# Other places for the side jobs of a unit, a re-ordered prologue, and gating and shared expert moved ahead in the last stages of an attention and mixture-of-experts layer

## The chip, the core and the metric

The kernel runs as one program on one core of one Trainium2 chip. The metric is the device time of one execution in microseconds (us). The engines are named as the profile names them: PE is TensorE (matmuls; its weight loads have a row of their own, PEld), DVE is VectorE, ACT is ScalarE, POOL is GpSimd, SP is SyncE, whose queue issues nearly all DMAs.

## The reference

One layer on x of 2048 tokens by 128 channels, all float32. The modulation rows sa, ca, ga, sb, cb, gb come from silu(c) @ wmod.

```python
h = layernorm(x) * (1 + ca) + sa
x = x + ga * attention(h)       # 16 heads; head n is tokens 128n..128n+127, reshaped to 2048 rows of 64
h = layernorm(x) * (1 + cb) + sb
x = x + gb * ffn(h)

# attention of a head: xq, xk, xv = h_block @ w.T, seen as 2048 x 64 each
out = softmax(xq @ xk.T / 8) @ xv           # then projected by wo

# ffn: gate by sigmoid(h @ gate_w.T) + expert_bias, top 2 of 8 experts, each token weighted by its score
# ahead of the expert and behind it; plus one shared expert for all tokens
h_e = (silu((w * h) @ w1[e].T) * ((w * h) @ w3[e].T)) @ w2[e].T * w
shared = silu(h @ sw1.T) * (h @ sw3.T) @ sw2.T
```

## The kernel before

The program is written engine by engine, each an in-order stream, tied by semaphores. It is fully unrolled and has three stages.

**Prologue.** Weights are loaded and transposed on PE (the setup jobs, list `SETUP`, copied out of PSUM by ACT), layer norm statistics of all 16 blocks of x are made by DVE, the first head is projected, and the first 20 "pairs" are done. A pair is a matmul of queries by keys into two PSUM banks (L1060) and a maximum over it on DVE (L870). The maxima give each row's softmax shift (`peak`, transposed on PE at L1071, stored by DVE, and spread by a DMA into `shifts`).

**Units.** Each of 16 heads has two halves of 1024 queries; a half is a unit, numbered 0 to 31. A unit has 32 places, four to a step. At the first two places of a step PE makes the scores of one key tile each (six matmuls of fp32r in row tiles of 64, L1113 to L1119), at the other two it multiplies an earlier tile of exponentials by v (L1137, fp32 in column tiles). ACT makes the exponentials (L738), POOL adds them up (L789, 15 adds of 128x1024 in a unit), which is the denominator. At set places there are side jobs for the next head or unit, written in the tables `LONG_JOBS`, `LOW_PLACES` and `SCALE_PLACES`, one dictionary for the first half and one for the second: q, k, v projections of the next head, a `sum` of the denominators of the unit before, its reciprocals on DVE in four parts (`inv`, L890) and the product with them (`scale`), the output projection `out` (L1161) of the head before, and `shift`. Twelve pairs of the next unit stand at the odd places 1 to 23, four of the unit after at 25 to 31. All side jobs on PE but the pairs use one PSUM bank, so each waits for the one before to be read out (`job_free`). In `side_jobs` the long jobs are put in first and the pairs behind them:

```python
    places = [[] for _ in range(4 * PAIRS)]
    for place, (kind, i) in LONG_JOBS[half].items():
        ...
    if pairs:
        for i in range(EARLY_PAIRS, PEAK_PAIRS):
            places[2 * (i - EARLY_PAIRS) + 1].append(("pair", i))
```

All pairs of the units use the same two banks, so a pair's matmul waits until DVE has reduced the one before.

**The last head and the feed-forward stage.** The last head (units 30 and 31) has no next head to project. In unit 31 DVE does the second layer norm of the 12 blocks that are ready (statistics, L322 for the normalization), PE transposes them (`turn`), makes the gate logits, and DVE picks the experts (`gate`, L492 to L509). Then come 36 items (4 groups of 512 tokens by 8 experts and, last of its group, the shared one). For each routed item PE spreads a row of token weights over all partitions by a matmul with a selecting matrix (`spread`, L391), ACT copies it out (`keep_spread`), POOL multiplies the tokens by it (L412), PE does w1 and w3 (L442, L443), ACT silu (L474), DVE two products (L532, L534), PE w2 (L424). The last four blocks' norm, gate and weights are done between items 2 and 8.

## Time and profile before

| | us |
|---|---|
| three runs | 1463.69, 1469.81, 1469.3 |
| median of them | 1469.3 |
| the profiled execution | 1464.93 |
| its span | 1463.1 |
| PE busy in the span | 1397.1 |
| POOL busy | 1186.8 |
| DVE busy | 929.7 |
| ACT busy | 679.9 |
| mean granted TensorE clock | 0.981 of full speed |

The span is what the profiler saw from the first instruction to the last; 1.8 us of the profiled execution's time lie around it. PE's busy time is near the span, but matmuls are pipelined and their ends are modelled, so it does not say that PE has nothing to give. The gaps between weight loads (PEld) are the finer tool.

### The profile page before, as it was taken

Reading aid. Unit: us, or ns where it says so; the run is one execution under the profiler, and the core shown is the slowest. Engines: PE = TensorE matmul, PEld = TensorE weight load, DVE = VectorE, ACT = ScalarE, POOL = GpSimd, SP = SyncE. Lnnn points to the kernel's source line nnn. Section 1 sums busy time; section 2 is a strip of 40 time slices with the busy share of each in tenths; the row PEclk is TensorE's granted clock in tenths of the full one; section 3 lists DMA queues with packets and bytes.
Section 4 is the critical chain, followed back from the end, with each engine's and each line's share of the span. In section 5 each row is a group of like instructions: output and inputs, shape, how many; then the busy total and the mean of one; then the engine's idle time right before and its main releaser. Section 6 shows DMA issues by size and latency. Waiting matters only on the chain.

```text
span 1463.1 us, 19932 instructions
## 1 busy us (share of the span) xinstructions
PE 1397.1 (95%) x7882; PEld 710.8 (49%) x7882; DVE 929.7 (64%) x1050; ACT 679.9 (46%) x849; POOL 1186.8 (81%) x534
## 2 busy tenths in 40 slices
PE   5899999999999999999999999999999999987998
PEld 4454545454454545454445454544545454443555
DVE  5666666666666665666666666666666666584544
ACT  5354444444444445444444444544445444453332
POOL 1299899898989898989989898989898999975232
PEclk8799999999999999999999999999999999998999
DMA  7010101010100101010101010000101010000000
GB/s 189 1 44 1 44 1 44 1 44 1 30 15 9 37 1 44 1 44 1 44 1 44 1 43 1 23 23 1 44 1 44 1 44 1 1 0 1 8 8 15
DMA packets 27279, 32.93 MB, mean 23 GB/s; under 512 B 3755, under 2 KB 14643, under 8 KB 27187
## 3 DMA queue, kind: packets, MB, share of 16 engines
q1 hardware_dynamic: 27042, 31.67, 9.1%
q8 instruction: 62, 1.02, 0.3%
q14 instruction: 31, 0.25, 0.1%
q10 hardware_dynamic: 144, 0.00, 0.0%
HBM read 5.31 MB, written 1.05 MB: 4 GB/s over the span
## 4 chain that ended last, share of the span: by engine, by line
PE 76%; DVE 13%; POOL 4%; ACT 4%; issue 3%; DMA 0%; SPq 0%; POOLq 0%; ACTq 0%; DVEq 0%
PE ps L1137 26%; PE ps L1060 13%; DVE peak_parts L870 7%; PE ps L1113 6%; PE ps L1119 6%; PE ps L1116 6%; PE ps L1039 5%; POOL acc L789 4%; PE ps L1042 2%; PE ps L442 2%; PE ps L1161 2%; DVE ps L890 2%; PE ps L424 2%; PE ps L443 2%; PE ps L1150 2%
## 5 line engine op out<-in xcount | busy, mean ns | idle before, releaser
L789 POOL TENSOR_TENSOR acc<-acc,probs 128x1024 f32<-128x1024 f32 x448 | 1065.4, 2378 | 124.1 <-ACT probs L738 68.8
L870 DVE TENSOR_REDUCE peak_parts<-ps 128x2 f32<-128x1024 f32 x512 | 622.6, 1218 | 365.8 <-PE ps L1060 362.1
L738 ACT ACTIVATE probs<-ps 128x1024 f32<-128x1024 f32 x512 | 496.6, 1022 | 455.7 <-PE ps L1119 375.7
L1137 PE MATMUL ps<-probs,v_sb 128*64 128x512 f32 x2048 | 502.0, 606 | 0.0
L1137 PEld LDWEIGHTS ps<-probs,v_sb 128*64 128x64 f32 x2048 | 124.4, 136 | 212.8 <-issue 170.2
L1113 PE MATMUL ps<-q_hi,d_swap_hi 64*128 64x512 f32 x512 | 201.7, 394 | 0.0
L1113 PE MATMUL ps<-q_hi,d_hi 64*128 64x512 f32 x512 | 201.5, 394 | 0.0
L1116 PE MATMUL ps<-q_lo,d_hi 64*128 64x512 f32 x512 | 200.2, 391 | 0.0
L1119 PE MATMUL ps<-q_hi,d_lo 64*128 64x512 f32 x512 | 200.1, 391 | 0.0
L1116 PE MATMUL ps<-q_lo,d_swap_hi 64*128 64x512 f32 x512 | 200.0, 391 | 0.0
L1119 PE MATMUL ps<-q_hi,d_swap_lo 64*128 64x512 f32 x512 | 199.9, 390 | 0.0
L1060 PE MATMUL ps<-k_swap_hi,q_hi 64*128 64x512 f32 x512 | 129.8, 504 | 8.2 <-DVE peak_parts L870 7.3
L1060 PE MATMUL ps<-k_hi,q_hi 64*128 64x512 f32 x512 | 125.8, 488 | 8.3 <-DVE peak_parts L870 6.0
L890 DVE RECIPROCAL ps<-ps 128x128 f32<-128x128 f32 x128 | 119.3, 947 | 19.3 <-PE ps L1150 19.3
L1060 PEld LDWEIGHTS ps<-k_swap_hi,q_hi 64*128 64x128 f32 x512 | 48.3, 185 | 134.9 <-DVE peak_parts L870 95.4
L412 POOL TENSOR_TENSOR probs<-hT,token_weights 128x512 f32<-128x512 f32 x32 | 40.7, 1274 | 80.5 <-PE ps L443 76.8
L789 POOL TENSOR_TENSOR acc<-probs 128x1024 f32<-128x1024 f32 x32 | 75.9, 2372 | 35.3 <-ACT probs L738 35.3
L1060 PEld LDWEIGHTS ps<-k_hi,q_hi 64*128 64x128 f32 x512 | 48.3, 185 | 110.0 <-DVE peak_parts L870 81.8
L1116 PEld LDWEIGHTS ps<-q_lo,d_hi 64*128 64x128 f32 x512 | 94.9, 185 | 12.7
L1113 PEld LDWEIGHTS ps<-q_hi,d_swap_hi 64*128 64x128 f32 x512 | 95.3, 186 | 10.6 <-issue 0.2
L1119 PEld LDWEIGHTS ps<-q_hi,d_lo 64*128 64x128 f32 x512 | 94.8, 185 | 11.5
L1119 PEld LDWEIGHTS ps<-q_hi,d_swap_lo 64*128 64x128 f32 x512 | 94.8, 185 | 10.6
(150 smaller groups left out, 1204.7 us busy)
## 6 DMA issues: line engine op xcount, KB each, us to landing
k_swap_hi<-k_hi SPq DMA_DIRECT2D x64, 128.0 KB, 2.3
d_swap_hi<-d_hi SPq DMA_DIRECT2D x64, 128.0 KB, 2.3
d_swap_lo<-d_lo SPq DMA_DIRECT2D x64, 128.0 KB, 2.3
probs<-in_L_ffn_w_dram SPq DMA_DIRECT2D x2, 512.0 KB, 5.2
shifts<-shift_sb SPq DMA_DIRECT2D x64, 2.0 KB
out_dram<-probs SPq DMA_DIRECT2D x4, 256.0 KB, 2.3
x_in<-in_L_attn_x_dram SPq DMA_DIRECT2D x1, 960.0 KB, 9.3
probs<-in_L_attn_wq_dram SPq DMA_DIRECT2D x1, 512.0 KB, 4.8
```

The lines of the kernel that those rows point to most:

```text
L412: pool.tensor_tensor(weighted[m % 2], hT[:, g * BANK:(g + 1) * BANK], token_weight[n % 4], ALU.mult).then_inc(weighted_ready, 1)
L424: mm = pe.matmul(ps[:, 6 + g % 2, k * P:(k + 1) * P], inner_w[m % 2][:, k * P:(k + 1) * P], w2T[:, e, :], start=(e == 0 and k == 0), stop= ...
L738: act.activation(probs[:, kt % PROBS, :], ps[:, 2 * place:2 * place + 2, :].rearrange("p a b -> p (a b)"), ACT.Exp, scale=SCALE).then_inc( ...
L789: pool.tensor_tensor(total, total if kt > 1 else probs[:, 0, :], probs[:, kt % PROBS, :], ALU.add).then_inc(added, 1)
L870: dve.tensor_reduce(peak_parts[:, :, i // STRETCHES, i % STRETCHES], ps[:, bank:bank + 2, :], AX.X, ALU.max).then_inc(peak_free, 1)
L890: dve.reciprocal(job.ps[:, cols], job.ps[:, cols]).then_inc(part_inverted, 1)
L1039: mm = pe.matmul(job.ps[:, k * P:(k + 1) * P], w[:, at:at + P], h_head[:, :], start=True, stop=True)
L1060: mm = pe.matmul(ps[:, bank + b, :], q_hi[at, target_parity, q:q + P], keys[at, target_parity, cols], start=True, stop=True, tile_position ...
L1113: pe.matmul(ps[:, slot + b, :], hi[b][at[b], p, cols], q_hi[at[b], p, q], start=kt < 2, stop=False, tile_position=(b * HEAD_DIM, 0), skip_ ...
L1116: pe.matmul(ps[:, slot + b, :], hi[b][at[b], p, cols], q_lo[at[b], p, q], start=False, stop=False, tile_position=(b * HEAD_DIM, 0), skip_g ...
L1119: mm = pe.matmul(ps[:, slot + b, :], lo[b][at[b], p, cols], q_hi[at[b], p, q], start=False, stop=kt >= 2, tile_position=(b * HEAD_DIM, 0), ...
L1137: mm = pe.matmul(ps[at:at + HEAD_DIM, PV_BANK, :], v_sb[:, p, chunk_of(kt) * HEAD_DIM:(chunk_of(kt) + 1) * HEAD_DIM], probs[:, kt % PROBS, ...
```

## The change

1. In `side_jobs` the long jobs of a place now stand behind its pair. `out` and the second `v` move from place 23 to 27, the reciprocals and `scale` of both halves to other places, `low k` one place later, ACT's rounding of a k step one place earlier. The wait that keeps `out`'s bank moves from the shift to whichever counted job comes next.
2. In the prologue the pairs come in another order (`PAIR_ORDER`), the v projections stand between pairs, the setup jobs are spread one to a pair from pair 2 to 17, the statistics of layer norm are taken as soon as x has landed, and several small operations leave DVE for ACT and POOL.
3. The second layer norm and the gating of 12 blocks are spread over both units of the last head (`LAST_HEAD_PLACES`); the normalization itself is on ACT (`norm_act`).
4. Token weights are no longer spread by PE and ACT. They are written to memory and read back by one broadcast DMA of 128x512 for each expert and group, into `token_weights`, which has now eight parts. The hi and lo parts of the weights, `select` and `weight_hi` are gone.
5. The shared expert is first of its group. The first items stand before the last unit's sum; sum, reciprocals, scale, projection and the norm and gate of the last four blocks stand between items 3 and 18. DVE weighs the tokens of items 1 and 2.

```diff
 LONG_JOBS = (
-    {3: ("q", 0), 6: ("sum", 0), 15: ("k", 0), 19: ("k", 1), 23: ("out", 0), 25: ("shift", 0)},
-    {3: ("q", 1), 7: ("v", 0), 10: ("sum", 0), 23: ("v", 1), 25: ("shift", 0)},
+    {3: ("q", 0), 15: ("k", 0), 19: ("k", 1), 25: ("shift", 0), 27: ("out", 0)},
+    {3: ("q", 1), 7: ("v", 0), 25: ("shift", 0), 27: ("v", 1)},
 )
+SUM_PLACES = (6, 10)
...
 SCALE_PLACES = (
-    {7: ("inv", 0), 8: ("inv", 1), 10: ("inv", 2), 11: ("inv", 3), 12: ("scale", 0)},
-    {10: ("inv", 0), 11: ("inv", 1), 14: ("inv", 2), 16: ("inv", 3), 17: ("scale", 0)},
+    {6: ("inv", 0), 7: ("inv", 1), 9: ("inv", 2), 11: ("inv", 3), 13: ("scale", 0)},
+    {10: ("inv", 0), 12: ("inv", 1), 15: ("inv", 2), 19: ("inv", 3), 21: ("scale", 0)},
 )
...
+LAST_HEAD_PLACES = (
+    {5: [("stats", 0)], 9: [("stats", 1)], 13: [("stats", 2)], 15: [("root", 0)], 17: [("rstd", 0)],
+     18: [("norm", 0)], 22: [("norm", 1)], 26: [("norm", 2)], 27: [("turn", 0), ("turn", 1)], 31: [("turn", 2)]},
+    {3: [("logits", 0)], 4: [("gate", 0)], 19: [("weights", 0), ("weights", 1), ("weights", 2)]},
+)
...
+        ORDER = [EXPERTS] + list(range(EXPERTS))
...
+        SUM_AFTER, INVERT_AFTER, SCALE_AFTER, PROJECT_AFTER, ADD_AFTER = 3, (3, 4), 5, 6, 6
+        STATS_AFTER, ROOT_AFTER, RSTD_AFTER, NORM_AFTER = 7, 8, 8, 9
+        GATE_AFTER = (13, 14, 15, 16)
+        LATE_AFTER = {10: ("turn", 3), 12: ("logits", 1), 18: ("weights", 3)}
...
             for m in range(ITEMS):
-                g, e = m // ALL, m % ALL
-                spread(pe, m + 2)
+                g, e = m // ALL, ORDER[m % ALL]
...
+        def spread_weights(sp, g):
+            sp.wait_ge(tail_free, tail("weights", g).full)
+            sp.dma_start(weights_dram[:, g * BANK:(g + 1) * BANK], weightT[g % 2]).then_inc(weights_out, 16)
+            sp.wait_ge(weights_out, 16 * (g + 1))
+            for e in range(EXPERTS):
+                if g > 0:
+
+                    sp.wait_ge(inner_w_ready, (g - 1) * ALL + ORDER.index(e) + 1)
+                sp.dma_start(token_weight[e], weights_dram[e:e + 1, g * BANK:(g + 1) * BANK].broadcast_to(
+                    [P, BANK])).then_inc(weights_loaded[e], 16)
```

On PE, at place 15 of a first half (the k projection), this stands in the order before. `probs,v_sb` is the product with v, `k_swap_hi,q_hi` a pair, `h_head,wkT` the projection, `d_hi` and `d_lo` scores:

```order
L1137 MATMUL ps<-probs,v_sb 64x512 x4
L1039 MATMUL ps<-h_head,wkT 128x128 x4
L1060 MATMUL ps<-k_swap_hi,q_hi 128x512 x2
L1113 MATMUL ps<-q_hi,d_hi 128x512
L1113 MATMUL ps<-q_hi,d_swap_hi 128x512
```

And this after the change:

```order
L1190 MATMUL ps<-probs,v_sb 64x512 x4
L1114 MATMUL ps<-k_swap_hi,q_hi 128x512 x2
L1093 MATMUL ps<-h_head,wkT 128x128 x4
L1166 MATMUL ps<-q_hi,d_hi 128x512
L1166 MATMUL ps<-q_hi,d_swap_hi 128x512
```

The pair, which stood between projection and scores, now stands between the product with v and the projection.

On DVE, in the same first half from the q residue on, `peak_parts` is the reduction of a pair, `RECIPROCAL` one part of the inverse, `oT` the scaling. Before:

```order
L850 TENSOR_TENSOR q_lo<-ps,q_hi 128x512
L870 TENSOR_REDUCE peak_parts<-ps 128x2 x2
L890 RECIPROCAL ps<-ps 128x128 x2
L870 TENSOR_REDUCE peak_parts<-ps 128x2
L890 RECIPROCAL ps<-ps 128x128
L870 TENSOR_REDUCE peak_parts<-ps 128x2
L890 RECIPROCAL ps<-ps 128x128
L897 TENSOR_TENSOR oT<-o_raw,ps 128x512
L870 TENSOR_REDUCE peak_parts<-ps 128x2 x2
```

After:

```order
L901 TENSOR_TENSOR q_lo<-ps,q_hi 128x512
L924 TENSOR_REDUCE peak_parts<-ps 128x2
L944 RECIPROCAL ps<-ps 128x128
L924 TENSOR_REDUCE peak_parts<-ps 128x2
L944 RECIPROCAL ps<-ps 128x128
L924 TENSOR_REDUCE peak_parts<-ps 128x2
L944 RECIPROCAL ps<-ps 128x128
L924 TENSOR_REDUCE peak_parts<-ps 128x2
L944 RECIPROCAL ps<-ps 128x128
L924 TENSOR_REDUCE peak_parts<-ps 128x2
L951 TENSOR_TENSOR oT<-o_raw,ps 128x512
```

No two reciprocals stand together any more, and the first one is ahead of the pair that it stood behind.

On PE, in the feed-forward stage, two routed items read so before (`q_hi,k_hi` is the spreading matmul):

```order
L391 MATMUL ps<-q_hi,k_hi 128x512
L442 MATMUL ps<-probs,w1T 128x512
L443 MATMUL ps<-probs,w3T 128x512
L424 MATMUL ps<-w2T,probs 128x128 x4
L391 MATMUL ps<-q_hi,k_hi 128x512
```

And so after the change:

```order
L439 MATMUL ps<-acc,w1T 128x512
L440 MATMUL ps<-acc,w3T 128x512
L425 MATMUL ps<-w2T,probs 128x128 x4
L439 MATMUL ps<-acc,w1T 128x512
L440 MATMUL ps<-acc,w3T 128x512
```

The spreading matmul is gone from PE; the weighted tokens lie in `acc` instead of `probs`.

## Rows read from the trace of the kernel before

**Rows 1.** Busy time by stretch: length, busy us of each engine, PEclk, DMA share, GB/s

```profile
0.00:63.00 63.00, 42.01 (x177) 27.75 (x179) 36.28 (x80) 28.08 (x54) 6.02 (x22) 0.76 0.42 110
...
294.30:335.40 41.10, 39.95 (x245) 20.83 (x243) 27.31 (x30) 19.74 (x25) 37.49 (x17) 1.00 0.17 39
335.40:373.20 37.80, 37.55 (x215) 17.58 (x213) 24.49 (x25) 17.92 (x22) 33.95 (x15) 1.00 0.00 1
1240.20:1276.40 36.20, 35.15 (x211) 17.17 (x209) 22.65 (x45) 16.07 (x18) 34.34 (x15) 1.00 0.00 1
1276.40:1317.50 41.10, 35.82 (x198) 17.16 (x196) 31.69 (x30) 21.65 (x24) 31.12 (x14) 0.92 0.00 0
...
1343.50:1463.10 119.60, 110.57 (x460) 66.72 (x459) 55.34 (x94) 43.18 (x70) 35.71 (x28) 0.98 0.03 9
```

**Rows 2.** PEld timeline, a step without side job: start, length, idle before in brackets

```profile
353.64 0.18 PEld L1060 LDWEIGHTS ps<-k_swap_hi,q_hi 64*128 64x128 f32 x2 [0.81 <-DVE peak_parts L870]
...
355.46 0.19 PEld L1060 LDWEIGHTS ps<-k_hi,q_hi 64*128 64x128 f32 x2 [0.35 <-DVE peak_parts L870]
355.90 0.20 PEld L1137 LDWEIGHTS ps<-probs,v_sb 128*64 128x64 f32 x4 [0.25 <-issue]
...
357.76 0.19 PEld L1060 LDWEIGHTS ps<-k_hi,q_hi 64*128 64x128 f32 x2 [0.81 <-DVE peak_parts L870]
```

**Rows 3.** PEld timeline, the q projection with its pair

```profile
297.21 0.97 PEld L1039 LDWEIGHTS ps<-h_head,wqT 128*128 128x128 f32 x8 [0.81 <-issue]
298.30 0.19 PEld L1060 LDWEIGHTS ps<-k_hi,q_hi 64*128 64x128 f32 x2
```

**Rows 4.** PEld timeline, unit 30, scores of two tiles with no pair beside

```profile
1271.70 0.18 PEld L1113 LDWEIGHTS ps<-q_hi,d_hi 64*128 64x128 f32 x1 [0.81 <-issue]
...
1273.29 0.20 PEld L1137 LDWEIGHTS ps<-probs,v_sb 128*64 128x64 f32 x4 [0.36 <-issue]
```

**Rows 5.** PEld timeline, unit 6: a late pair, and a k projection that waits

```profile
307.86 0.19 PEld L1060 LDWEIGHTS ps<-k_hi,q_hi 64*128 64x128 f32 x2 [1.27 <-DVE peak_parts L870]
...
317.61 0.97 PEld L1039 LDWEIGHTS ps<-h_head,wkT 128*128 128x128 f32 x8 [1.12 <-DVE d_lo L864]
```

**Rows 6.** PEld timeline, unit 6: last pair, shift, first early pair

```profile
325.12 0.19 PEld L1060 LDWEIGHTS ps<-k_swap_hi,q_hi 64*128 64x128 f32 x2
...
327.22 0.08 PEld L1071 LDWEIGHTS ps<-ident,peak 128*8 128x8 f32 x1 [0.65 <-issue]
327.45 0.19 PEld L1060 LDWEIGHTS ps<-k_hi,q_hi 64*128 64x128 f32 x2
```

**Rows 7.** DVE timeline, unit 6: two reciprocals in a row

```profile
304.96 1.77 DVE L890 RECIPROCAL ps<-ps 128x128 f32<-128x128 f32 x2
```

**Rows 8.** POOL timeline: adds of unit 7, and the last ten of unit 31

```profile
346.88 27.58 POOL L789 TENSOR_TENSOR acc<-acc,probs 128x1024 f32<-128x1024 f32 x11 [0.29 <-ACT probs L738]
...
1302.32 27.08 POOL L789 TENSOR_TENSOR acc<-acc,probs 128x1024 f32<-128x1024 f32 x10 [7.50 <-ACT probs L738]
```

**Rows 9.** DVE timeline of the prologue: the first reductions

```profile
25.04 3.48 DVE L870 TENSOR_REDUCE peak_parts<-ps 128x2 f32<-128x1024 f32 x3
```

**Rows 10.** Groups of DVE from 1277 to 1320: busy us, mean ns, idle before

```profile
L500 DVE TENSOR_TENSOR wkT<-wvT 128x768 f32<-128x768 f32 x1 | 3.1, 3140 | 0.0
...
L499 DVE TENSOR_TENSOR wqT<-wvT 128x768 f32<-128x768 f32 x1 | 1.0, 957 | 0.0
```

**Rows 11.** PEld timeline, feed-forward stage: w1 of items 12, 13, 34 and 35

```profile
1383.81 0.30 PEld L442 LDWEIGHTS ps<-probs,w1T 128*128 128x128 f32 x2 [0.24 <-issue]
...
1387.05 0.30 PEld L442 LDWEIGHTS ps<-probs,w1T 128*128 128x128 f32 x2 [0.24 <-issue]
...
1452.41 0.30 PEld L442 LDWEIGHTS ps<-probs,w1T 128*128 128x128 f32 x2
...
1455.02 0.30 PEld L442 LDWEIGHTS ps<-hT,w1T 128*128 128x128 f32 x2
```

**Rows 12.** DMA issues on the page: queue, count, KB each, median us to landing

```profile
out_dram<-probs SPq DMA_DIRECT2D x4, 256.0 KB, 2.3
```

More of the change, by code:

```diff
@@ L70, in chunk_of, with side_jobs @@
     return half * 8 + pair * 2 + odd
-def side_jobs(half, sums=True, project=True, pairs=True, early=True, last_unit=False):
+def side_jobs(half, sums=True, project=True, pairs=True, early=True, last_head=False):
     places = [[] for _ in range(4 * PAIRS)]
-    for place, (kind, i) in LONG_JOBS[half].items():
-        if sums if kind in ("sum", "out") else pairs if kind == "shift" else project:
-            places[place].append((kind, i))
+    if sums:
+        places[SUM_PLACES[half]].append(("sum", 0))
     if pairs:
@@ L84, in side_jobs @@
             places[2 * (PEAK_PAIRS - EARLY_PAIRS + i) + 1].append(("pair", i))
+    for place, (kind, i) in LONG_JOBS[half].items():
+        if sums if kind == "out" else pairs if kind == "shift" else project:
+            places[place].append((kind, i))
     if project:
@@ L90, in side_jobs @@
             places[place].append(job)
-    if last_unit:
-        for place, job in LAST_UNIT_JOBS.items():
-            places[place].append(job)
+    if last_head:
+        for place, jobs in LAST_HEAD_PLACES[half].items():
+            places[place] += jobs
     return [places[4 * step:4 * step + 4] for step in range(PAIRS)]
@@ L552, in ffn_store @@
                              x_out[g % 2].rearrange("p (b d) -> p b d", d=DIM)).then_inc(stored[g % 2], 16)
+            for g in range(3):
+                spread_weights(sp, g)
+            store(0)
+            spread_weights(sp, 3)
+            for g in range(1, GROUPS):
+                store(g)
             for n in (0, 1):
@@ L747, in body @@
                                     sums.append(jobs_at(t) + local + 1)
-                                if kind in ("turn", "logits"):
+                                if kind in ("turn", "logits", "weights"):
                                     gating_act(act, kind, i)
+                                if kind == "root":
+                                    layernorm_root(act, range(READY_BLOCKS), 5)
+                                if kind == "norm":
+                                    norm_act(act, range(4 * i, 4 * i + 4), 2)
                                 local += kind in COUNTED
@@ L752, in body @@
                             copy_pv(unit, sums[-1] if sums else None)
-                        if step == 1 and last_head and half == 1:
-                            layernorm_root(act, range(READY_BLOCKS), 3)
             pairs_of_heads(body)
             copy_pv(UNITS, sums[-1])
-            for kind, i in EPILOGUE:
-                gating_act(act, kind, i)
-            keep_spread(act, 0)
-            keep_spread(act, 1)
             ffn_act(act)
@@ L964, in _ @@
             pairs_of_heads(body)
[L965 to L969 removed]
+            ffn_dve(dve, link, invert, scale_outputs, add_head)
         @block.tensor
@@ L1220, in body @@
                                     project(head - 1, job)
+                                    heads_out = head
                                 if kind == "shift":
-                                    turn_shift(job, unit + 1, head if half == 0 and not first else None)
-                                if kind in ("turn", "logits"):
+                                    turn_shift(job, unit + 1)
+                                if kind in ("turn", "logits", "weights"):
                                     tail_job(kind, i)
```

365 lines of the change are left out of this document (185 added, 180 removed).

## The prediction

> **What bounds the kernel now.** I read the busy times by stretch first. The stages are the prologue to 63 us, 32 units, and the feed-forward stage; PE is busy nearly throughout a unit, POOL is next [rows 1]. A first half is 41.1 us long (unit 6) and a second half 37.8 (unit 7), so a head takes 78.8. Then I read the weight loads of PE one by one, since busy time hides waits. A step without side job is 353.64 to 357.76 = 4.12 us: from the pair behind the products to the pair behind the scores 1.82, then 0.44 to the first product with v, then 1.86 for the two products [rows 2]. The 1.82 holds a wait for DVE: the two pairs share their banks, and a reduction takes 1.2 us (3.48 for three) [rows 9]. POOL's adds follow each other at 27.58 / 11 = 2.52 (with their gap) [rows 8], 15 of them 37.8: a floor of 75.6 for a head. POOL therefore hardly lags in the mean, and PE sets the head, 3.2 us above that floor. In the prologue PE is granted 0.76 of its clock in the mean, a mixture of its levels 1.2 and 2.4 GHz [rows 1], and the first reduction starts at 25.04 [rows 9].
>
> **Steady units, a job behind its pair.** The surprise to look for is that the swap in itself gives next to nothing. Before, q takes 1.09 (297.21 to 298.30) and is followed by its pair, whose reduction is due 1.82 later [rows 2, 3]: from q to the product with v 1.09 + 1.82 + 0.44 = 3.35. After it, the pair comes first and costs 0.44 until a full-array matmul can load (as pair to product [rows 2]), q 1.09, then scores of two tiles. Those without any pair took 1271.70 to 1273.29 = 1.59 for six row-tiled pairs of loads, to the next product [rows 4]; one more adds about (1.59 - 0.44) / 5 = 0.23. Sum 0.44 + 1.09 + 1.59 + 0.23 = 3.35. DVE now reduces the pair while q runs, but PE drains between tilings once more, and the two cancel. I take 0 for each of q, k, k, out, q, v, v (seven per head); the bounds are a gain of 0.23 (no extra drain) and a loss of 0.44 (drain, and no wait hidden).
> The Trainium skill (TensorEngine Tiling, Key Properties) says that changing the tiling mode drains the TensorE. The trace agrees where a lone row-tiled pair costs 0.44 instead of 0.23. By that rule alone the change would lose 7 x 0.2 per head, about 20 us.
>
> **Steady units, waits that go.** (a) DVE does two reciprocals in a row, 1.77, ahead of a due reduction [rows 7]; the pair at 307.86 has 1.27 of idle time instead of 0.81 as a normal one [rows 2, 5], so 0.46. After it no two stand together, the first runs in the slack before place 7, and each leaves its reduction inside the 2.3 us until the next pair behind the products: 0.46 per first half. (b) The second k waits for the low part of the first: idle 1.12 for 0.81, so 0.31 [rows 5], and `out` likewise for the second. Now the job stands 0.44 behind its pair and `out` four places later: 0.62 per first half. (c) From the last pair to the first early one 2.33 (325.12 to 327.45), with the shift's transpose 0.23 of it and waiting for the maximum [rows 6]. With the early pair first: 1.82 for it, 0.44, transpose 0.23 to the product = 2.49; before 2.33 + 0.43 = 2.76. Saved 0.27 in every unit. The rounding of k ahead of an exponential costs nothing: PE needs that one only a step later.
> First halves save 0.46 + 0.62 + 0.27 = 1.35, second halves 0.27. Units 2 to 28 hold 14 first, units 1 to 29 hold 15 second halves: 18.9 + 4.1 = 23.0. Unit 0 loses about 0.5: its second pair now comes straight behind the first and waits for DVE about 1.1 with nothing between, against 0.31 + 0.27 saved. **Sum of the units: -22.5.** A head then takes 77.2, still over POOL's floor of 75.6, which would allow 3.2 a head, 48 in 15 heads; the change takes 23 of them.
>
> **Prologue.** Reductions start when DVE is through with the statistics. Those move ahead of the q residue, into time in which DVE waited, and DVE gives up about ten small operations. I estimate the first reduction at about 21 instead of 25.04 [rows 9]. Twenty of 1.2 us are at least 24, so scores could start at 45 at best, against 61; PE, at its low level for half of this stretch [rows 1], does a pair and a setup job in about 1.8 there. I take -8, with -3 (only the earlier start) and -15 (DVE bound throughout) as ends.
>
> **Last head.** Unit 30 was 36.2, unit 31 41.1 [rows 1], with POOL standing 7.50 for want of exponentials before its last ten adds, which end at 1302.32 + 27.08 = 1329.4, 89.2 behind the start of unit 30 [rows 1, 8]. Now the statistics, the norm's factors and the gate lie on DVE beside POOL's adds. There a DVE product of 128x768 took 3140 ns beside an add, and the same size 957 without [rows 10]: such an operation waits for the add's end. The three statistics (about 1.2 each) and the factors delay reductions, so unit 30 grows by about 7 to 43.5. Unit 31 loses the 7.50 at the norm, but the gate, some 21 us of such operations from place 4 on, ends 7 us after PE gets to place 19, where the weights' transposes wait for it and all scores behind them. I let POOL's last add end 92 behind the start of unit 30: **+3**, ends -6 and +12.
> The Trainium skill (GPSIMD Engine Reference, Specifications) says that GpSimd shares its SBUF interfaces with DVE instructions of two SBUF inputs. The 3140 against 957 ns agree, so moving the gate to an earlier place buys no faster gate.
>
> **Feed-forward stage.** From POOL's last add to the end it was 1463.1 - 1329.4 = 133.7. Now items 0 to 2 fit before that add is over, since DVE weighs 1 and 2; item 3 starts 1.4 after it. A routed item's pace was 3.24 (1383.81 to 1387.05) with the spreading matmul and 2.61 (1452.41 to 1455.02) without [rows 11]. The 2.61 is the loop silu, two DVE products, w2, so I take it for all 32 paces: 83.5. Into them go sum, projection, turn, logits and weights on PE, about 5.3, and reciprocals, factors, gate pieces and two changes of activation table beyond the idle time of DVE and ACT, about 4. The last item is a routed one, with one product more: 8.1 + 0.7 = 8.8. Sum 1.4 + 83.5 + 5.3 + 4 + 8.8 = 103.0, so **-30.7**; ends -38 and -15 (pace 3.1). I give back 2 for PE at its low level behind the wait at place 19.
> The broadcasts: 8 for a group, in the 23 us that the group before takes, and 256 KB landed in 2.3 [rows 12], so they are hidden.
>
> **The sum.** -22.5 - 8 + 3 - 30.7 + 2 = -56.2 from the profiled execution: span 1463.1 to 1406.9, time 1464.93 to 1408.7. The median of the runs is 4.4 above the profiled time and the lowest run 1.2 below it; I predict **1409**.
>
> **Rivals.**
> 1. The extra drains are not cancelled. If each of the seven jobs costs 0.12 more, 105 jobs in units 1 to 29 cost 12.6: 1422; at 0.44, 46: 1455. For it: one run more of row-tiled matmuls each time. Against: the three rows add up to the same 3.35. 0.14.
> 2. The end stages give little: POOL's last add 12 late and a pace of 2.9 for 2.61 (+9) make 1409 + 9 + 9 = 1427. For it: DVE and POOL share their time in the last head; the pace of 2.61 is seen only on single items. 0.14.
> 3. More: the prologue bound by DVE (-7) and 7 less in the stages behind: 1395. 0.09.
> 4. Slower than before: the broadcasts come one after the other and set the pace. They would have to take (103 + 56) / 32 = 5.0 us each; at less than 2.6 they hide. A store of 256 KB took 2.3 from issue to landing [rows 12], but one source row is read 128 times here. 1475 or more. 0.02.
> 5. The steady units do not change, as POOL sets them after all: 1409 + 22.5 = 1431. Against: POOL waited for exponentials before the adds of unit 7 [rows 8]. 0.04.
> The forecast itself has 0.57, and its own range is 1400 to 1420.
>
> **How the numbers follow.** The range 1395 to 1434 takes in rivals 2, 3 and 5 and rival 1 up to 0.24 per job, and leaves out about 2 in 10. A measurement of this kernel tells about 0.5% (7 us) from no change; for the median to stay in 1462 to 1477, rival 1 and 2 would have to hold together. Faster 0.96, same 0.02, slower 0.02.
>
> **What would show it.** Half units of about 39.7 and 37.5 us between first exponentials; no idle time beyond 0.81 ahead of a projection or `out`; from a pair behind the products to a projection 0.44; the first scores near 53; place 19 of unit 31 waiting for DVE; items at 2.6. The prediction is wrong if projections cost over 1.2 behind their pair, if DVE's products of the gate pile up beyond 25 us, or if broadcasts end an item's wait.

## The result, and the profile after

The changed kernel takes 1388.3 us in the median of four runs (1388.0 to 1389.6), and the kernel before, on the same chip, 1467.5: a ratio of 0.946, 95% interval 0.944 to 0.948. The forecast was 1409 with a range of 1395 to 1434, and the result lies outside it. The direction was right, and 20 us of gain were missed. The profiled execution took 1388.47, its span is 1386.7.

The stages, by the busy times of the stretches (columns as in [rows 1]): prologue, unit 6, unit 7, unit 30, unit 31, and from POOL's last add to the end.

```profile
0.00:48.40 48.40, 36.44 (x177) 25.61 (x179) 33.98 (x71) 29.57 (x58) 7.04 (x27) 0.90 0.56 143
276.50:316.00 39.50, 39.50 (x243) 20.79 (x243) 27.44 (x30) 19.43 (x24) 37.41 (x16) 1.00 0.18 41
316.00:353.50 37.50, 37.50 (x215) 17.56 (x213) 24.39 (x25) 17.85 (x22) 33.78 (x15) 1.00 0.00 1
1200.20:1238.50 38.30, 36.55 (x223) 18.36 (x221) 23.09 (x48) 25.64 (x35) 36.29 (x16) 1.00 0.00 1
1238.50:1270.80 32.30, 32.07 (x190) 16.14 (x190) 19.80 (x17) 16.80 (x20) 28.60 (x12) 0.95 0.15 31
1284.80:1386.70 101.90, 95.32 (x440) 59.54 (x440) 54.53 (x94) 28.10 (x45) 38.13 (x31) 0.95 0.25 69
```

Against [rows 1] every stage but unit 30 is shorter; unit 30 now holds work that unit 31 had. ACT's timeline has the exact starts, here of the first exponential of units 0, 6 and 7 (those of 8, 30 and 31 are at 353.50, 1200.17 and 1238.52):

```profile
48.41 1.02 ACT L786 ACTIVATE probs<-ps 128x1024 f32<-128x1024 f32 x1 [3.55 <-PE ps L1178]
...
276.53 1.94 ACT L786 ACTIVATE probs<-ps 128x1024 f32<-128x1024 f32 x2 [2.03 <-PE ps L1178]
...
316.01 1.94 ACT L786 ACTIVATE probs<-ps 128x1024 f32<-128x1024 f32 x2 [2.21 <-PE ps L1178]
```

| stage of the profiled execution | forecast | measured |
|---|---|---|
| prologue (63.1 to 48.4) | -8 | -14.7 |
| units 0 to 29 (1177.1 to 1151.8) | -22.5 | -25.3 |
| unit 30's start to POOL's last add (89.2 to 84.7) | +3 | -4.6 |
| POOL's last add to the end (133.7 to 101.9) | -30.7 | -31.8 |
| clock | +2 | 0, lies in the stages |
| sum | -56.2 | -76.4 |

**The swap on PE.** PEld's timeline of unit 6: a pair, q behind it, the next pair, the first product with v (compare [rows 2, 3]); then the last pair of this unit and the first early one with the shift's transpose behind it ([rows 6]).

```profile
279.43 0.19 PEld L1114 LDWEIGHTS ps<-k_hi,q_hi 64*128 64x128 f32 x2 [0.81 <-DVE peak_parts L924]
279.86 0.97 PEld L1093 LDWEIGHTS ps<-h_head,wqT 128*128 128x128 f32 x8 [0.25 <-issue]
...
282.22 0.19 PEld L1114 LDWEIGHTS ps<-k_swap_hi,q_hi 64*128 64x128 f32 x2
282.77 0.20 PEld L1190 LDWEIGHTS ps<-probs,v_sb 128*64 128x64 f32 x4 [0.37 <-issue]
...
304.13 0.19 PEld L1114 LDWEIGHTS ps<-k_swap_hi,q_hi 64*128 64x128 f32 x2 [0.81 <-DVE peak_parts L924]
305.96 0.19 PEld L1114 LDWEIGHTS ps<-k_hi,q_hi 64*128 64x128 f32 x2 [0.35 <-DVE peak_parts L924]
306.39 0.08 PEld L1122 LDWEIGHTS ps<-ident,peak 128*8 128x8 f32 x1 [0.24 <-issue]
306.59 0.20 PEld L1190 LDWEIGHTS ps<-probs,v_sb 128*64 128x64 f32 x4
```

From pair to product it is 282.77 - 279.43 = 3.34, where the prediction had built 3.35 for both orders. The pair behind q no longer waits for DVE, and what that saves goes into the change of tiling. At the shift 304.13 to 306.59 is 2.46, forecast 2.49.

**The prologue.** DVE's timeline: the first reductions and some of the later ones. They start at 20.31 and not at 25.04 [rows 9]; the three from 29.92 on start 1.13 apart.

```profile
20.31 3.48 DVE L924 TENSOR_REDUCE peak_parts<-ps 128x2 f32<-128x1024 f32 x3
...
29.92 3.48 DVE L924 TENSOR_REDUCE peak_parts<-ps 128x2 f32<-128x1024 f32 x3
```

**The last head.** DVE's and POOL's timelines of unit 31 around the gate. POOL's one stand is 2.41 (before, 7.50 in [rows 8]), and the gate falls into it.

```profile
1244.43 0.21 DVE L502 TENSOR_SCALAR wvT<-wvT 128x96 f32<-128x96 f32 x1 [11.66 <-ACT wvT L461]
...
1245.76 0.96 DVE L509 TENSOR_TENSOR wqT<-wvT 128x768 f32<-128x768 f32 x1
1246.64 0.95 DVE L510 TENSOR_TENSOR wkT<-wvT 128x768 f32<-128x768 f32 x1
1247.62 3.01 DVE L512 TENSOR_TENSOR wkT<-wkT,earlier 128x768 f32<-128x768 f32 x1
1250.67 3.01 DVE L514 TENSOR_TENSOR wqT<-wqT,wkT 128x768 f32<-128x768 f32 x1
...
1256.04 0.26 DVE L518 TENSOR_TENSOR wvT<-wvT 128x96 f32<-128x96 f32 x1
```

```profile
1246.77 38.07 POOL L851 TENSOR_TENSOR acc<-acc,probs 128x1024 f32<-128x1024 f32 x14 [2.41 <-ACT probs L786]
1284.80 2.48 POOL L413 TENSOR_TENSOR acc<-hT,token_weights 128x512 f32<-128x512 f32 x2
```

**The feed-forward stage.** PEld's timeline of two items, with w1 at 1359.62 and 1362.23: a pace of 2.61, as it is in all plain items, the routed ones of [rows 11] having had 3.24.

```profile
1359.62 0.30 PEld L439 LDWEIGHTS ps<-acc,w1T 128*128 128x128 f32 x2
...
1361.02 0.19 PEld L425 LDWEIGHTS ps<-w2T,probs 128*128 128x128 f32 x1 [0.24 <-issue]
...
1362.23 0.30 PEld L439 LDWEIGHTS ps<-acc,w1T 128*128 128x128 f32 x2
```

None of this item's idle time is put down to another engine. In some items the idle time ahead of w2 is 0.35 instead of 0.24 and put down to DVE's product, at the same pace. The one long wait of the stage is for POOL's first product (L413), ahead of item 3, as PEld's timeline shows:

```profile
1286.11 0.50 PEld L439 LDWEIGHTS ps<-acc,w1T 128*128 128x128 f32 x2 [4.85 <-POOL acc L413]
```

### The profile page after: what moved, and what is told of

It reads as the page before. It is cut to its first block, busy times and chain, and to the rows that moved or that the text cites. A ratio compares the mean times of both kernels' runs of the same rounds, so it can differ in the third digit from the quotient of the medians.

```text
span 1386.7 us, 19883 instructions
## 1 busy us (share of the span) xinstructions
PE 1361.5 (98%) x7850; PEld 697.3 (50%) x7850; DVE 908.4 (66%) x1023; ACT 663.7 (48%) x837; POOL 1186.4 (86%) x537
## 3 DMA queue, kind: packets, MB, share of 16 engines
q8 instruction: 62, 1.02, 0.3%
## 4 chain that ended last, share of the span: by engine, by line
PE 93%; POOL 3%; DVE 2%; ACT 1%; issue 0%; DMA 0%; SPq 0%; POOLq 0%; DVEq 0%
PE ps L1190 33%; PE ps L1114 14%; PE ps L1166 10%; PE ps L1172 8%; PE ps L1169 8%; PE ps L1093 5%; POOL acc L851 2%; PE ps L1096 2%; PE ps L1214 2%; PE ps L425 2%; PE ps L439 2%; PE ps L440 2%; PE ps L1203 2%; DVE peak_parts L924 1%; PE ps L1178 1%
## 5 line engine op out<-in xcount | busy, mean ns | idle before, releaser
L786 ACT ACTIVATE probs<-ps 128x1024 f32<-128x1024 f32 x512 | 502.5, 1029 | 394.6 <-PE ps L1172 326.2
L1166 PE MATMUL ps<-q_hi,d_hi 64*128 64x512 f32 x512 | 213.0, 416 | 0.0
L1166 PE MATMUL ps<-q_hi,d_swap_hi 64*128 64x512 f32 x512 | 212.9, 416 | 0.0
L1114 PE MATMUL ps<-k_hi,q_hi 64*128 64x512 f32 x512 | 121.8, 472 | 5.1 <-DVE peak_parts L924 2.6
L1114 PE MATMUL ps<-k_swap_hi,q_hi 64*128 64x512 f32 x512 | 120.9, 469 | 2.2 <-DVE peak_parts L924 2.0
L1166 PEld LDWEIGHTS ps<-q_hi,d_hi 64*128 64x128 f32 x512 | 94.9, 185 | 36.3 <-issue 24.9
L1169 PEld LDWEIGHTS ps<-q_lo,d_swap_hi 64*128 64x128 f32 x512 | 95.1, 186 | 9.7
```

Of the source, the lines that this page charges most:

```text
L786: act.activation(probs[:, kt % PROBS, :], ps[:, 2 * place:2 * place + 2, :].rearrange("p a b -> p (a b)"), ACT.Exp, scale=SCALE).then_inc( ...
L1114: mm = pe.matmul(ps[:, bank + b, :], q_hi[at, target_parity, q:q + P], keys[at, target_parity, cols], start=True, stop=True, tile_position ...
L1166: pe.matmul(ps[:, slot + b, :], hi[b][at[b], p, cols], q_hi[at[b], p, q], start=kt < 2, stop=False, tile_position=(b * HEAD_DIM, 0), skip_ ...
L1169: pe.matmul(ps[:, slot + b, :], hi[b][at[b], p, cols], q_lo[at[b], p, q], start=False, stop=False, tile_position=(b * HEAD_DIM, 0), skip_g ...
```

## Experiments in the steady units

All are edits of the changed kernel. Half units were read between first exponentials, as above, at units 2 to 5 and 28, 29, which agree within 0.1.

**Jobs ahead of their pairs again.**

```diff
+    for place, (kind, i) in LONG_JOBS[half].items():
...
     if pairs:
         for i in range(EARLY_PAIRS, PEAK_PAIRS):
...
-    for place, (kind, i) in LONG_JOBS[half].items():
...
```

> The changed kernel with each long job ahead of the pair of its place again, all tables of places as changed. Theory (the swap in itself gives nothing for q, k, v and out; the shift's transpose gives 0.27 in every unit, and the second k meets the low part of the first again, 0.3): first halves 39.48 to 40.1, second halves 37.48 to 37.75, together 14 x 0.6 + 15 x 0.27 = 12, so 1400. Rival A (each switch between row-tiled and full-array matmuls costs 0.2 that nothing hides): this kernel saves 7 x 0.2 per head and the shift's and k's losses stay, 12 - 21 = -9, so 1379. Rival B (the swap lets VectorE reduce under every job and gives 0.2 per job): 12 + 21, so 1421.

Measured 1403.2 (ratio to before 0.957, 0.954 to 0.959). First halves 40.20, second 37.78; units 0 to 29 take 1165.5 instead of 1151.8. The units cost 13.7 more where the theory has 12, and the time is 3.2 above the theory's 1400; both rivals fall. Of the 0.72 that a first half loses, 0.31 is the shift's, as in second halves. PEld's timeline of unit 6 has 0.12 ahead of the second k, less than expected (idle time 0.93 for 0.81), and 0.23 ahead of the first k, which waits for the scaling (1.04).

**Reciprocals together.**

```diff
-    {6: ("inv", 0), 7: ("inv", 1), 9: ("inv", 2), 11: ("inv", 3), 13: ("scale", 0)},
+    {7: ("inv", 0), 8: ("inv", 1), 10: ("inv", 2), 11: ("inv", 3), 12: ("scale", 0)},
```

> The changed kernel with the reciprocals of a first half at the old places 7, 8, 10, 11 and the scaling at 12, nothing else. Theory (two in a row, 1.8 us, delay a due reduction by 0.46 per first half): first halves 39.94, second halves 37.48 as they are, 14 x 0.46 = 6.4, so 1394.7. Rival (with the pair ahead of its job the reduction is no longer waited for there): no change, 1388.

Measured 1404.5 (0.958, 0.955 to 0.960): 16 more, not 6.4. First halves are 40.50, second 37.48. DVE's timeline of unit 6, first of this kernel, then of the changed kernel, in the stretch of the reciprocals:

```profile
289.81 1.77 DVE L944 RECIPROCAL ps<-ps 128x128 f32<-128x128 f32 x2
...
294.50 0.95 DVE L944 RECIPROCAL ps<-ps 128x128 f32<-128x128 f32 x1
295.48 0.69 DVE L951 TENSOR_TENSOR oT<-o_raw,ps 128x512 f32<-128x512 f32 x1
296.08 1.22 DVE L924 TENSOR_REDUCE peak_parts<-ps 128x2 f32<-128x1024 f32 x1
```

```profile
287.19 0.96 DVE L944 RECIPROCAL ps<-ps 128x128 f32<-128x128 f32 x1
288.05 1.16 DVE L924 TENSOR_REDUCE peak_parts<-ps 128x2 f32<-128x1024 f32 x1
```

The late reductions hold back PE's next pair twice, as PEld's timeline of this kernel shows with 1.26 and 1.24 of idle time where 0.81 is normal:

```profile
292.70 0.19 PEld L1114 LDWEIGHTS ps<-k_hi,q_hi 64*128 64x128 f32 x2 [1.26 <-DVE peak_parts L924]
...
297.36 0.19 PEld L1114 LDWEIGHTS ps<-k_swap_hi,q_hi 64*128 64x128 f32 x2 [1.24 <-DVE peak_parts L924]
```

The first delay is the forecast 0.46. The second comes where the scaling (0.69) follows a reciprocal: it too is two long operations in a row, 1.67, and ahead of k's pair the changed kernel has them apart. It costs 1.24 - 0.81 = 0.43. With k ahead of that pair (the last experiment of this section) it costs nothing: k's own idle time is 0.81 there. The 1.02 is these two delays and 0.11 at the pair between them (0.48 for 0.37).

**Output projection and second v at place 23 again.**

```diff
-    {..., 19: ("k", 1), 25: ("shift", 0), 27: ("out", 0)},
-    {..., 7: ("v", 0), 25: ("shift", 0), 27: ("v", 1)},
+    {..., 19: ("k", 1), 23: ("out", 0), 25: ("shift", 0)},
+    {..., 7: ("v", 0), 23: ("v", 1), 25: ("shift", 0)},
```

> The changed kernel with the output projection and the second v at place 23 again, still behind their pairs. Theory (the projection waits for the low part of the second k, 0.31 per first half; v loses nothing): first halves 39.8, second halves 37.48, 14 x 0.31 = 4.3, so 1392.7. Rival (behind its pair the projection already stands late enough): no change, 1388. Rival (the move apart of projection and shift by itself costs or gives in the last step, 6.48 us now): first halves change by some tenths though the projection has no idle time for VectorE.

Measured 1387.7 (0.946, 0.944 to 0.948), halves 39.5 and 37.47: no difference. This is the first rival: behind its pair the projection already stands late enough, so the new place adds nothing to the swap.

**All tables of places as before, only the swap left.** The edit puts the old tables back (the reciprocals' and projections' as above, `low k` at 17 and 21, and the second half's reciprocals at 10, 11, 14, 16). ACT's rounding of a k step stays one place earlier, so this is not the swap quite alone.

> The changed kernel with all tables of places as before (reciprocals two in a row, low parts of k at 17 and 21, projection and second v at 23), so that of the change in the steady units only the order of job and pair is left. Measured so far: two reciprocals in a row cost 1.03 per first half behind swapped jobs, the place of the projection nothing; before the halves were 41.03 and 37.78. Theory (the swap gives what the prediction gave it, the shift's 0.27 and, through k and the projection that no longer wait for VectorE, 0.3 in first halves): halves 40.5 and 37.5, 1388 + 15 = 1403. Rival (much of the gain is the new places and the swap is worth nothing in first halves): 41.0 and 37.5, 1410.

Measured 1403.1 (0.957, 0.956 to 0.959), halves 40.49 and 37.47: the theory. PEld's timeline of unit 6 says what became of the waits. First the kernel before: `out`, which waited for the low part of k as the second k did ([rows 5], 1.12):

```profile
323.13 1.86 PEld L1161 LDWEIGHTS ps<-wo,oT 128*128 128x128 f32 x16 [1.12 <-DVE d_lo L864]
```

Then this kernel: the pair that the scaling delays, the second k and `out`:

```profile
295.73 0.19 PEld L1114 LDWEIGHTS ps<-k_swap_hi,q_hi 64*128 64x128 f32 x2 [1.24 <-DVE peak_parts L924]
...
301.34 0.97 PEld L1093 LDWEIGHTS ps<-h_head,wkT 128*128 128x128 f32 x8 [0.25 <-issue]
...
306.55 1.86 PEld L1214 LDWEIGHTS ps<-wo,oT 128*128 128x128 f32 x16 [0.25 <-issue]
```

Both waits of 0.31 are gone by the swap, and the delay of 0.43 by the scaling, which the old order hid, has come.

**Jobs ahead of pairs and reciprocals together** is the missing corner:

> The changed kernel with jobs ahead of pairs and the reciprocals of a first half two in a row again, low parts of k and the projection at their new places. Jobs ahead alone cost 0.71 per first half, reciprocals alone 1.03. Theory (the second reciprocal costs 1.03 only where the job behind it stands late, and 0.46 as in the prediction where it stands first): first halves 40.21 + 0.46 = 40.67, 1403 + 7 = 1410. Rival (the two losses add up): first halves 41.24, 1418.

Measured 1409.3 (0.961, 0.960 to 0.963), halves 40.53 and 37.78: the theory, a little under it. The four corners and before:

| first half / second half | pair first | job first |
|---|---|---|
| reciprocals apart | 39.48 / 37.48 (changed) | 40.20 / 37.78 |
| reciprocals together | 40.50 / 37.48 | 40.53 / 37.78 |
| all tables old | 40.49 / 37.47 | 41.03 / 37.78 (before) |

So with the old tables the swap gives 0.54 and 0.31, and spreading the reciprocals gives 1.02 when the pair stands first but 0.33 when the job does. Neither is worth alone what it is worth beside the other. The places of `low k` and `out` (with ACT's earlier rounding) show the same: they give nothing when the pair stands first and 0.50 when the job does, 0.31 of it ahead of `out` and 0.19 ahead of the second k.

## Experiments in the prologue

**The old order, with early statistics.**

```diff
-        PAIR_ORDER = [0, 1, 4, 5, 2, 3] + list(range(6, PEAK_PAIRS + EARLY_PAIRS))
+        PAIR_ORDER = list(range(PEAK_PAIRS + EARLY_PAIRS))
...
```

`PROLOGUE` is pairs 0 to 7, second q, pairs 8 to 15, shift, both v, pairs 16 to 19 again.

> The changed kernel with the old order of the prologue on every engine: pairs in their natural order, the shift behind pair 15, both v and the last four pairs behind the shift. The statistics stay early. First exponential now at 48.41. Theory (the early statistics bring 4.7 of the 14.7, and the v products, each about 2.5 with their copies at PE's low level, now stand inside the time in which VectorE reduces): the first reduction stays at 20.3, and the first exponential comes 7 to 10 later, 55.4 to 58.4; the rest unchanged, so 1395 to 1398. Rival (nearly all of it came from the earlier start and the clock): first exponential within 2 of 48.4.

Measured 1394.4 (0.950, 0.948 to 0.952). The first exponential comes at 55.54, 7.1 later; the first reduction at 20.95. The granted clock is at 0.50 from 23 to 33 and from 47 to 57 us, where the changed kernel has it from 22 to 29 and from 46 to 49. How much of the 7.1 is the order itself and how much this lower clock, the run does not say.

**Late statistics, with the new order.**

```diff
-            dve.wait_ge(x_loaded, 16)
-            layernorm_sums(dve, x_in, range(1, BLOCKS)).then_inc(sums_ready, 1)
...
-                if (kind, i) == ("k", 0):
-                    dve.wait_ge(sums_ready, 1)
-                    layernorm_moments(dve, range(1, BLOCKS))
-                if (kind, i) == ("low k", 0):
+                if (kind, i) == ("pair", 0):
+                    dve.wait_ge(x_loaded, 16)
+                    layernorm_stats(dve, link, x_in, range(1, BLOCKS))
```

ACT's root of the variances and DVE's factors (`layernorm_rstd`) stand there too.

> The changed kernel with the layer norm's statistics of blocks 1 to 15 (sums, moments, root) back ahead of the first pair on VectorE and ScalarE, and the new order of the prologue kept. Theory (every reduction is moved by the start, VectorE bound behind it): first reduction at 24 to 25 instead of 20.31, first exponential 4 to 5 later, 52.4 to 53.4, so 1392 to 1393. Rival (the longer idle time of PE ahead of the pairs lowers its granted clock for longer: before it was 0.50 from 24 to 42 us, after it only to 29): first exponential 8 or more later, low level past 35 us, 1396 or more.

Measured 1393.0 (0.949, 0.947 to 0.952). First reduction 25.13, first exponential 53.03, 4.6 later. In the profiled execution unit 0 also took 40.2 at a granted clock of 0.87, against 36.7 at 0.99 in the changed kernel. The start's share is as expected; the rival's longer low level did not come where it said (the level was back at 1.00 by 36) but behind the prologue.

**PE kept busy, too coarsely.**

```diff
+                    if i in (1, 2):
+                        for _ in range(6 if i == 1 else 3):
+                            pe.matmul(ps[:, 3, :], h_head[:, :], wqT[:, 0:BANK], start=True, stop=True)
```

> The changed kernel with nine matmuls of 128x512 more on PE (into a bank that the second q overwrites), six ahead of the second pair and three ahead of the third, where PE idles 2.39 and 0.64 us while VectorE is busy. Their results are not used. Theory (PE's idle time between 18 and 22 us is what lowers its clock from 22 to 29 us, where a pair and a transpose take 1.77 instead of 1.2): granted clock 1.00 throughout 20 to 40 us, first exponential 1.5 to 2.5 earlier, 1386. Rival (the clock falls regardless of it, or transfers and copies set the pace there): first exponential within 0.5, or later because the extra matmuls lie on the path.

Measured 1388.4 (0.946, 0.943 to 0.948), no gain, and the profiled execution was the longest of four, 1393.5. The granted clock was 1.00 from 18 to 46, as the theory says. But an fp32 matmul takes two passes of 0.43, so the nine took about 8 us, and DVE waited 2.38 and 1.97 for pairs behind them: the first exponential came at 50.72. Then the clock fell at 47 and stayed at 0.50 to 61, and unit 0 took 40.1. A finer version stands at the end.

## Experiments in the last stages

**Norm and gate together again.** The tables of the last head, first and second half, become:

```python
    {},
    {4: [stats 0 to 2, root, rstd, norm 0 to 2], 8: [turn 0], 9: [turn 1], 10: [turn 2],
     11: [logits 0], 12: [gate 0], 31: [weights 0 to 2]},
```

> The changed kernel with the last head's side work put together again: statistics, root, factors and norm of 12 blocks all at place 4 of unit 31, turns and logits at 8 to 11, gate at 12, weights at 31; the feed-forward stage as changed. Theory (the work itself is small, what cost was that everything behind place 4 waited for it and POOL stood without exponentials): unit 30 is 36 to 36.5 long instead of 38.35, unit 31 longer by 10 or more, POOL's last add 89 to 91 behind the start of unit 30 instead of 84.7, and items 1 and 2 wait for the gate beside the adds: 1396 to 1402. Rival (the place is of no matter, since PE must do the same work): within 3 of 1388.

Measured 1397.4 (0.953, 0.950 to 0.955). Unit 30 is 35.25 long instead of 38.35, and POOL then stands 4.72 and 3.90 in unit 31, as its timeline shows; its last add ends at 1291.0, 90.0 behind the start of unit 30:

```profile
1252.43 7.35 POOL L852 TENSOR_TENSOR acc<-acc,probs 128x1024 f32<-128x1024 f32 x3 [4.72 <-ACT probs L787]
1263.69 27.33 POOL L852 TENSOR_TENSOR acc<-acc,probs 128x1024 f32<-128x1024 f32 x10 [3.90 <-ACT probs L787]
```

The granted clock is 0.84 in unit 31. The run moves the norm and the gate at once and does not tell their shares.

**The gate at place 10.**

```diff
-    {3: [("logits", 0)], 4: [("gate", 0)], 19: [...]},
+    {3: [("logits", 0)], 10: [("gate", 0)], 19: [...]},
```

> The changed kernel with the gate at place 10 of unit 31 instead of 4, all else as changed. It takes 11.9 now (1244.43 to 1256.29), with two of its four comparisons at 0.95 while POOL stands 2.41, and two at 3.01 beside an add. Theory (what such an operation takes hangs on whether POOL adds at that moment): behind place 10 POOL adds without pause, so all four take about 3.0, the gate 16 in all, it ends at 1264 or later, and PE waits for it at place 19 for 4 to 6: 1392 to 1395. Rival (3.01 and 0.95 are the prices of the operations themselves, by their shapes): the gate takes 11.9 again, ends at about 1260, and costs 1 at most: 1388 to 1389.

Measured 1392.8 (0.950, 0.947 to 0.952). DVE's timeline, for which POOL adds without pause from 1246.76 to 1268.25:

```profile
1255.04 1.75 DVE L504 TENSOR_TENSOR wvT<-wvT,bias_sb 128x96 f32<-128x96 f32 x1
1256.82 3.20 DVE L509 TENSOR_TENSOR wqT<-wvT 128x768 f32<-128x768 f32 x1
1259.94 3.09 DVE L510 TENSOR_TENSOR wkT<-wvT 128x768 f32<-128x768 f32 x1
```

The same L509 and L510 that took 0.96 and 0.95 take 3.20 and 3.09, the addition of the bias 1.75 for 0.26. The gate lasts 16.8 us (1253.81 to 1270.59), and PE stands 10.94 ahead of the weights' transposes. The price is the moment's, not the operation's, as the theory says. PE stands longer than the 4 to 6 that it gives, and the time, 4.5 more, is in its range. What counts is whether an add is running when the operation starts. In the changed kernel L510 starts at 1246.64, 0.13 ahead of POOL's add, and takes 0.95 beside it. L512 starts at 1247.62 within that add, which ends at 1249.82, and ends at 1250.63. The Trainium skill (GPSIMD Engine Reference, Specifications) says that GpSimd contends for its SBUF interfaces with VectorE instructions of two SBUF inputs; the rows agree. The prediction drew from the 3140 and 957 ns that an earlier place buys no faster gate, and that conclusion was wrong: at the earlier place POOL happened to stand.

**One matmul more per item.**

```diff
+                if m >= 12:
+                    pe.matmul(banks(m)[0], w1T[:, e, :], rhs, start=True, stop=True)
                 pe.matmul(banks(m)[0], w1T[:, e, :], rhs, start=True, stop=True)
```

> The changed kernel with the product with w1 done twice in items 12 to 35 of the feed-forward stage (one fp32 matmul of 128x512 more, two passes of 0.43 as the present ones). Theory (PE sets the pace of 2.61: four passes of 0.43 and eight of 0.112 are 2.61): pace 3.47, 24 x 0.86 = 20.6, so 1409. Rival (the loop of silu, two products of VectorE and w2 sets it, as the prediction said, and PE has room): pace up by less than 0.4, 1398 or less.

Measured 1408.3 (0.961, 0.958 to 0.963), 20.0 more. PEld's timeline shows items 3.46 apart, with no wait for another engine:

```profile
1331.00 0.30 PEld L440 LDWEIGHTS ps<-acc,w1T 128*128 128x128 f32 x2
...
1334.46 0.30 PEld L440 LDWEIGHTS ps<-acc,w1T 128*128 128x128 f32 x2
```

PE sets the pace. The prediction had the right 2.61 and the wrong owner.

**Every broadcast twice.**

```diff
...
+                sp.dma_start(spare[:, n % 2, :], weights_dram[e:e + 1, g * BANK:(g + 1) * BANK].broadcast_to(
+                    [P, BANK])).then_inc(spare_in[n % 2], 16)
                 sp.dma_start(token_weight[e], weights_dram[e:e + 1, g * BANK:(g + 1) * BANK].broadcast_to(
```

> The changed kernel with every broadcast of 256 KB in the feed-forward stage issued a second time, into two spare buffers in turn that nobody reads. Theory (the transfers hide: a group of eight has about 23 us, and each lands about 3.3 after its issue): pace of the items 2.61 as now, no item waits for a transfer, 1388 to 1389; at most the first group's, which are waited for at 1266.58, come some us later and cost 1 to 3. Rival (the forecast's rival 4, the transfers follow each other and are near the bound): pace over 2.61 and 1395 or more.

Measured 1390.9 (0.949, 0.947 to 0.951), 2.6 more. The pace is 2.61 up to item 29; from item 30 on, items come 3.1 apart in the mean, since POOL waits for transfers (11.0 us in six waits). The busy times from 1309 to 1364.5, of this kernel, have the DMA engines busy 0.87 of the time at 151 GB/s:

```profile
1309.00:1364.50 55.50, 55.50 (x266) 35.62 (x265) 30.95 (x54) 19.84 (x33) 23.43 (x18) 1.00 0.87 151
```

The changed kernel has 0.35 and 93 there. A broadcast lands 3.3 after its issue, and 7.9 when doubled. The transfers are hidden as forecast, but with less than a factor of two to spare: the rival needed 5.0 us each, and the last group shows about 3.1 for two.

## A version that is faster than both

**Item 3 weighed by DVE.**

```diff
-        FIRST_WEIGHED = (1, 2)
+        FIRST_WEIGHED = (1, 2, 3)
...
-            for m in FIRST_WEIGHED:
+            for m in FIRST_WEIGHED[:2]:
...
+                if m == 1:
+                    weigh_tokens(dve, 3, weighted_first)
```

> The changed kernel with item 3's tokens weighed by VectorE too, behind its products of item 1, instead of by POOL behind its last add; PE now waits 4.85 for that (to 1286.11), part of the rest at its low level. Theory (this wait is on the path): item 3 starts at 1282 to 1283, the sum straight behind POOL's last add at 1284.9 instead of 1289.8, everything behind it 3 to 4.5 earlier: 1384 to 1385. Rival (POOL's last add and its first product, 1284.8 to 1286.1, hold back the sum and item 4 just as well): at most 1 earlier, 1387 to 1388.

Measured 1383.9 (0.944, 0.941 to 0.946). PEld's timeline:

```profile
1285.04 0.30 PEld L439 LDWEIGHTS ps<-acc,w1T 128*128 128x128 f32 x2 [1.79 <-DVE acc L413]
```

Item 3 starts at 1285.04, 2 us later than the theory said, since DVE's product is done only then. Item 4 starts at 1288.85, 14.33 behind item 0, where the changed kernel has 18.56. The wait is on the path, and the time is the theory's. Part of the 4.2 is the clock: in the changed kernel's profiled execution it is at 0.51 from 1284.9 to 1291.8, here at 1.00. In the profiled execution with `out` at place 23, whose last stages are the changed kernel's and whose clock is low for only half as long there, item 4 stands 16.93 behind item 0. Between it and this kernel are 2.6.

**Item 3, and PE kept busy only where it idles.** Beside the edit above, matmuls of so many columns ahead of these pairs, and of 128 ahead of the shift:

```diff
+            BUSY_BEFORE = {1: (896, 0), 2: (384, 0), 14: (64, 6), 15: (64, 6), 16: (64, 6), 18: (64, 7), 19: (384, 7)}
...
+                    pe.matmul(ps[:, 3, 0:n], ident[:, :], wqT[:, 0:n], start=True, stop=True)
```

> The changed kernel with item 3 weighed by VectorE (measured alone: 4.5 faster) and, in the prologue, small matmuls with unused results only where PE idles: 896 and 384 columns ahead of the second and third pair, 64 ahead of pairs 14, 15, 16 and 18, 128 ahead of the shift, 384 ahead of pair 19 (the earlier nine of 512 were fp32, two passes each, took 8 us and held the pairs back). Theory (PE's idle time ahead of 22 us and of 46 us is what lowers the granted clock): clock 1.00 from 20 to 60, first exponential 1.5 to 3 earlier than 48.5, unit 0 at 36 to 36.7 always, so 1380 to 1382. Rival (the clock falls near 46 us all the same): first exponential within 1 of 48.5 and 1384.

Measured 1380.2 (1379.1 to 1382.7; 0.942, 0.940 to 0.944): 3.7 below the version before, and 8 below the changed kernel. The runs of the version before went from 1381.9 to 1385.0, so the two ranges meet, and the 3.7 rest on the traces too. The busy times of prologue and unit 0:

```profile
0.00:45.80 45.80, 37.15 (x195) 25.31 (x197) 33.56 (x71) 29.34 (x58) 7.05 (x27) 1.00 0.59 151
45.80:82.00 36.20, 34.87 (x215) 18.18 (x215) 23.31 (x24) 19.05 (x24) 30.88 (x13) 1.00 0.19 44
```

The granted clock is at its upper level up to 1376.5, the first exponential comes at 45.83, and unit 0 takes 36.2. Against the changed kernel's 48.41 and 36.7, matmuls whose results nobody reads are worth 2.6 us in the prologue and about 0.6 in unit 0, if they stand only in idle time.

## Why the prediction was too slow

**Steady units, -22.5 against -25.3: the mechanism held, each term a little small.** That q gives nothing by the swap is confirmed (3.34 against 3.35). Against rival 1, jobs ahead of pairs are slower, 1403, so the drains are covered. The shift's 0.27 is 0.31 in second halves, where it stands alone. Of the first half's 1.55 the rows place 1.48: 0.31 for the shift, 0.62 for the waits of k and `out`, as forecast, and 0.55 for the reciprocals, forecast as 0.46, since the pair behind the late one was 0.09 late as well. The corner table seems to say otherwise, 1.02 for the reciprocals and 0.54 for the swap. But 0.43 of this is the delay by the scaling, which the kernel before did not have: the swap alone brings it, and spreading the reciprocals takes it away. The prediction did not see it and did not need it. Unit 0 lost 0.9 instead of 0.5; about 0.6 of it is the lower clock at its start, since at the upper level (the fastest version) it takes 36.2, 0.3 over the kernel before.

**Prologue, -8 against -14.7: a term mis-sized.** The step that failed is that PE "does a pair and a setup job in about 1.8 there", taken for half of the stretch. This holds only at the low level (pairs at 23.34 and 25.11, 1.77 apart), which ended at 29 us and not at 43 as before. Behind it DVE set the pace, 1.13 for a reduction. Taken away one at a time, the early statistics are worth 4.6 and the order, by which the v products stand between pairs, 7.1, lower clock included. Before, the two v products ran from 52.65 to 57.36 at the low level, and DVE had nothing to reduce, as its timeline shows:

```profile
58.12 4.62 DVE L870 TENSOR_REDUCE peak_parts<-ps 128x2 f32<-128x1024 f32 x4 [5.62 <-PE ps L1060]
```

The remaining 3.0 has no run of its own, and the two need not add up. The measured value is next to the end of -15 that the prediction named for a prologue bound by DVE.

**Last head, +3 against -4.6: two steps failed, unit 30's 7 us and the gate's 21.** The larger is unit 30: 43.5 forecast, 38.35 measured. The three statistics and the factors were to delay reductions by 7. Beside the kernel with none of this work in unit 30 (35.25) they cost 3.1 together with PE's transposes, and PE's waits for reductions grew by only 1.6 (7.5 against 5.9). The rest is in unit 31: the forecast has 48.5 from its start to POOL's last add, and it was 46.3. The gate took 11.9 and not 21, since two of its comparisons and the addition of the bias ran in POOL's stand or ahead of its add, and PE's transposes at place 19 did not wait for it (idle time 0.81). At place 10, beside adds, it took 16.8, so even there 21 was too much. The kernel before had shown it: the same ten operations took 14.0 there (1300.67 to 1314.69), and 18.9 with the three for hi and lo that the change drops. Not every operation waits for an add: the reduction L516 starts at 1253.71 within one and takes 0.95. But being small does not free one: L517, 128x96, took 1.30 there and 0.21 at place 10, where POOL stood by then.

**Feed-forward stage, -30.7 against -31.8.** The terms held, one by one: item 3 starts 1.3 behind POOL's last add (forecast 1.4), from it to the last item are 91.8 (83.5 + 5.3 + 4 = 92.8), and the last item takes 8.8. The pace was right though its reason was wrong: it is PE's own. What the prediction did not have is that PE stands 4.85 ahead of item 3, because items 1 and 2 are done well before POOL's last add.

**Clock, +2 against nothing.** The 2 were for a low level behind a wait at place 19 that did not come. Low levels came elsewhere, from 1244.0 to 1247.5 and from 1284.9 to 1291.8. Still the granted clock is 0.992 over the span after 0.981, mostly because the prologue's low stretches got shorter: before they were from 22 to 43 and from 53 to 63 us.

What came is nearest to rival 3, with 0.09: the prologue near DVE's bound (-14.7 where it has -15) and less in the stages behind, 13.5 where it has 7. Its 1395 was still 7 too slow.

## What to carry to other kernels

Moving a job behind or ahead of another is worth what the engines around it wait for at that place, and two such edits need not be worth the sum of their parts. Run the corners before crediting one, and read the waits row by row: a corner can hold a delay that neither kernel has. A VectorE operation of two SBUF inputs had no price of its own here, 0.95 or 3.0 for the same one; look up what GpSimd does at that moment, at the new place, and what the same chain took in the kernel before. Where PE idles for a few microseconds ahead of a dense stretch, look at its granted clock behind it, and try small matmuls in the gap, no longer than the gap is.
